# A ViT block with mixture of experts on one core: keys spread by ScalarE, value sums in column halves, a shorter routing chain, warm-up matmuls and a new order of steps

## The reference

```python
h = patches(x) @ W.T + b                           # 1152 tokens, 768 -> 192
# attn: a two-way time mix (wkv) and a channel mix
z = layernorm(h)
a = ln(z, w1, b1); k, v, sr = a @ Wk.T, a @ Wv.T, sigmoid(a @ Wr.T)
y = bi_wkv(decay / T, first / T, k, v)             # scans along the 36 tokens, both ways
z = z + (sr * y) @ Wo.T
c = ln(z, w2, b2)
h = h + z + sigmoid(c @ Wrf.T) * (square(relu(c @ Wkf.T)) @ Wvf.T)
# ffn: 12-head attention (head size 16), then 8 experts, the best 2 per token
z = layernorm(h); q, k, v = ln(z) @ qkv_w.T + qkv_b
z = z + softmax(q @ k.T / 4) @ v @ proj_w.T + proj_b
n = ln(z)
top, index = top_k(n @ w_gate, 2); gates = softmax(top)
moe = sum over the 2 experts e of gate * (gelu(n @ W1[e] + b1[e]) @ W2[e] + b2[e])
return h + z + moe
```

## Time and profile before

| | us |
|---|---|
| median of 3 runs (400.06, 400.08, 402.23) | 400.08 |
| the profiled execution | 396.91 |
| its span from first to last instruction | 395.1 |
| TensorE busy in the span | 319.4 |
| VectorE busy | 250.4 |
| ScalarE busy | 149.0 |
| GpSimd busy | 88.3 |

### The profile page before, as it was taken

The page is one execution under the profiler, slowest core; times in us unless marked ns, Lnnn a source line. Parts: engine busy times, 40 slices in busy tenths (PEclk is TensorE's granted clock), DMA queues, the critical chain, the costliest instruction groups (busy, mean ns, idle before and its releaser), DMA issues.

```text
span 395.1 us, 6068 instructions
## 1 busy us (share of the span) xinstructions
PE 319.4 (81%) x2039; PEld 287.0 (73%) x2039; DVE 250.4 (63%) x585; ACT 149.0 (38%) x352; POOL 88.3 (22%) x88
## 2 busy tenths in 40 slices
PE   3959901884798979999999998559299999999990
PEld 3948801573586958888898787548199999999980
DVE  1527998999899877675778898578413233322230
ACT  0054501331725056476824764230223333333320
POOL 9310002000110110110001000006405555555631
PEclk9989955576999999999999999658589999999996
DMA  8950000000000021243506687100402222222322
GB/s 271 359 150 2 1 0 0 2 0 0 1 2 1 0 64 32 70 152 108 151 15 200 168 219 220 40 2 0 120 21 42 42 40 41 41 40 41 51 24 22
DMA packets 20554, 27.25 MB, mean 69 GB/s; under 512 B 3458, under 2 KB 15570, under 8 KB 20522
## 3 DMA queue, kind: packets, MB, share of 16 engines
q1 hardware_dynamic: 16634, 22.80, 19.5%
q0 software_dynamic: 3888, 4.03, 6.9%
HBM read 22.05 MB, written 4.77 MB: 68 GB/s over the span
## 4 chain that ended last, share of the span: by engine, by line
PE 65%; DVE 18%; ACT 6%; issue 5%; DMA 3%; POOL 1%; DVEq 0%; SPq 0%; ACTq 0%; POOLq 0%
PE banks L1230 11%; PE banks L1231 10%; PE banks L1438 9%; PE banks L1427 7%; PE banks L1429 7%; PE banks L1300 6%; PE banks L1351 4%; PE banks L1253 3%; ACT ht L681 2%; PE banks L1324 2%; PE banks L1340 2%; PE banks L1263 1%; DVE patch L1144 1%; DMA patch<-in_xp 1%; DVE arena L921 1%
## 5 line engine op out<-in xcount | busy, mean ns | idle before, releaser
L574 POOL TENSOR_TENSOR rs<-va,consts 96x6 f32<-96x6 f32 (+1 forms) x16 | 18.1, 1132 | 221.5 <-DVEq L880 117.3
L1194 DVE TENSOR_SCALAR s<-banks,ffn 128x192 f32<-128x192 f32 x20 | 8.3, 417 | 57.4 <-PE banks L1438 57.1
L606 POOL DMA_INDIRECT out<-s,ffn x20 | 31.7, 1587 | 52.2 <-DVE s L1194 49.5
L821 ACT ACTIVATE ffn<-banks 128x384 f32<-128x384 f32 x40 | 19.6, 490 | 63.1 <-PE banks L1429 63.1
L1438 PE MATMUL banks<-arena,ffn 128*128 x240 | 42.1, 326 | 0.0
L1438 PEld LDWEIGHTS banks<-arena,ffn 128*128 128x128 f32 x240 | 38.5, 190 | 0.0
L1253 PE MATMUL banks<-arena,patch 128*96 128x192 f32 x144 | 25.9, 342 | 6.0 <-DMA patch<-in_xp 6.0
L1263 PE MATMUL banks<-consts,xh 96*128 96x96 f32 (+1 forms) x96 | 12.8, 279 | 21.8 <-DVEq L898 21.7
L1253 PEld LDWEIGHTS banks<-arena,patch 128*96 128x96 f32 x144 | 24.8, 173 | 6.7 <-issue 5.9
L1263 PEld LDWEIGHTS banks<-consts,xh 96*128 96x128 f32 (+1 forms) x96 | 10.7, 146 | 24.5 <-DVEq L898 23.3
L1230 PE MATMUL banks<-ht,kvrw 128*128 128x288 f32 x40 | 17.2, 518 | 12.3 <-ACT ht L681 6.4
(11 more groups left out here) (216 smaller groups left out, 766.7 us busy)
## 6 DMA issues: line engine op xcount, KB each, us to landing
arena<-in_w SPq DMA_DIRECT2D x8, 576.0 KB, 5.3
patch<-in_xp SPq DMA_DIRECT2D x12, 288.0 KB, 5.9
arena<-in_w1a SPq DMA_DIRECT2D x8, 384.0 KB, 3.9
vs<-v_scratch SPq DMA_DIRECT2D x24, 114.8 KB
arena<-in_w1b SPq DMA_DIRECT2D x8, 195.0 KB
v_scratch<-vt SPq DMA_DIRECT2D x4, 229.5 KB, 2.9
xh_scratch<-xh SPq DMA_DIRECT2D x4, 216.0 KB, 2.2
out<-h SPq DMA_DIRECT2D x1, 864.0 KB, 4.8
```

The costliest lines, as they stand in the source:

```text
L606: pool.indirect_dma_start(out[:, :], bass.IndirectOffsetOnAxis(ap=IS[:, j:j + 1], axis=0), YG[j % 2], None, compute_op=ALU.add).then_inc(s ...
L821: freed(A(HST[j % 2][:, 384 * i:384 * (i + 1)], ps[:, 0:384], ACT.Gelu), job)
```

## The change

- `spread` becomes `spread:b:g` on ScalarE: for each head one ACTIVATE from PSUM with scale = head mask (a column of `head0` or `head1`) and bias = KB, the masked key bias that VectorE computes once at the start. The key copies KT, `ke_ready` and VectorE's spread go; scores wait for the banks of k and qk1.
- `pv`: two matmuls per slab, one for each image, into the column halves; VectorE's `weighted` normalises both images at once.
- Routing: wider masks, sums in other layouts, rounding by adding and subtracting `WHOLE`, ranks accumulated in one PSUM region, RT in one operation, ONEB 8 rows by ScalarE and 16 in four wide operations by VectorE, GpSimd no longer takes part. The gather indices are written first, straight from PSUM, and have a semaphore of their own.
- `up`: the expert's number is loaded after the matmuls, not before.
- Four warm-up matmuls on zeros before the first tok.
- A new `ORDER`. Unused: `ON_ACT` stays empty, the `BY_ACT` lines don't change what runs.

```diff
 ORDER = """
 tok:0 tok:1 tok:2 stats:a:0 apply:a:0 tok:3 tok:4 tok:5 stats:a:1 apply:a:1 turn:a:0 kvr:0:0 turn:a:1 kvr:0:1 wkv:0:0
-kvr:2:0 wkv:0:1 wexp:0:0 kvr:1:1 wexp:0:1 wexp:0:2 wkv:0:2 kvr:1:0 wkv:0:3 wexp:0:3 wexp:0:4 wkv:0:4 wkv:0:5 tok:6
-tok:7 tok:8 tok:9 tok:10 kvr:2:1 tok:11 stats:a:2 stats:a:3 apply:a:2 apply:a:3 turn:a:2 kvr:0:2 turn:a:3 wkv:0:6
-kvr:0:3 wkv:1:0 wkv:1:1 wkv:1:2 wexp:1:0 wexp:1:1 wexp:1:2 wo:0 wo:1 kvr:1:3 kvr:2:2 kvr:2:3 hx:0 hx:1 stats:2:0
-apply:2:0 wexp:1:3 kvr:1:2 wkv:1:3 stats:2:1 turn:2:0 wkv:1:4 apply:2:1 wexp:1:4 wkv:1:5 kf:0:0 kf:1:0 rv:0 rv:1 rv:2
-wkv:1:6 ff:0 stats:b:0 turn:2:1 kf:0:1 kf:1:1 rv:3 rv:4 rv:5 apply:b:0 wo:2 wo:3 hx:2 hx:3 turn:b:0 vt:0 qk:0 vl:0:0
-vl:1:0 stats:2:2 apply:2:2 turn:2:2 kf:0:2 kf:1:2 stats:2:3 apply:2:3 turn:2:3 spread:0 s:0 exp:0 s:1 exp:1 ff:1 rv:6
...
+wkv:0:1 wexp:0:0 wexp:0:1 kvr:1:0 wexp:0:2 wexp:0:3 kvr:1:1 wkv:0:2 wexp:0:4 wkv:0:3 wkv:0:4 wkv:0:5 tok:6 tok:7 tok:8
+tok:9 tok:10 tok:11 stats:a:2 stats:a:3 apply:a:2 apply:a:3 kvr:2:0 kvr:2:1 wkv:0:6 turn:a:2 turn:a:3 kvr:0:3 kvr:0:2
+wkv:1:0 wo:0 wo:1 stats:2:0 hx:0 kvr:2:2 hx:1 wkv:1:1 wkv:1:2 apply:2:0 wexp:1:0 wexp:1:1 wexp:1:2 wexp:1:3 kvr:1:3
+kvr:1:2 wkv:1:3 turn:2:0 wexp:1:4 wkv:1:4 wkv:1:5 stats:2:1 kvr:2:3 kf:0:0 kf:1:0 rv:0 rv:1 apply:2:1 turn:2:1 wkv:1:6
+rv:2 ff:0 stats:b:0 apply:b:0 kf:0:1 kf:1:1 rv:3 wo:2 wo:3 turn:b:0 qk:0 spread:0:0 spread:1:0 hx:2 hx:3 stats:2:2
+apply:2:2 vt:0 vl:0:0 rv:4 rv:5 turn:2:2 s:0 exp:0 s:1 exp:1 vl:1:0 ff:1 stats:b:1 kf:0:2 kf:1:2 vm:0:0 pt:0 pt:1
...
         def _(act):
...
-                    if g:
-                        act.wait_ge(ke_ready, g)
-                    ps = full(act, ("k", g))
-                    freed(A(KT[:, 0, :], ps[:, 0:GT], ACT.Identity, bias=chan_("k_b", 0)), ("k", g))
                     ps = full(act, ("qk1", g))
                     A(QT[0:C1, g % 2, 1, 0:GT], ps[0:C1, 0:GT], ACT.Identity, bias=chan_("q_b", 1))
-                    freed(A(KT[0:C1, 1, :], ps[C1:2 * C1, 0:GT], ACT.Identity, bias=chan_("k_b", 1)), ("qk1", g))
+                if kind == "spread":
+                    b = step[1]
+                    heads, rows, lo, job = ((8, 128, 0, ("k", g)), (4, C1, C1, ("qk1", g)))[b]
...
+                    for h in range(heads):
+                        ins = A(ke[:, :, h, :], src, ACT.Identity, bias=KB[0:rows, 8 * b + h:8 * b + h + 1],
+                                scale=const_(f"head{b}", rows)[:, h:h + 1])
+                    freed(ins, job)
...
+            act.wait_ge(bb_ready, 1)
+            for i in range(NACT):
+                A(ONEB[:, i, :], const_("iota", T), ACT.Abs, bias=BB[:, i:i + 1], scale=-1.0).then_inc(apart_ready, 1)
+            for i in range(NACT):
+                act.wait_ge(apart_ready, i + 1)
+                A(ONEB[:, i, :], ONEB[:, i, :], ACT.Relu, bias=1.0, scale=-1.0).then_inc(table2_ready, 1)
...
         def _(dve):
...
+            dve.memset(O[:, :, :], 0.0).then_inc(warm_ready, 1)
...
+            dve.wait_ge(loaded["const"], 16)
+            for b, heads in ((0, 8), (1, 4)):
+                TS(KB[:, 8 * b:8 * b + heads], const_(f"head{b}"), CH[:, VAT["k_b"] + b:VAT["k_b"] + b + 1], None, ALU.mult).then_inc(kb_ready, 1)
...
             def weighted(p):
-                for a in range(2):
-                    r = slice(64 * a, 64 * a + 64)
-                    ins = TTR(O[r, p % 2, :].rearrange("p (h d) -> p h d", h=NH), ps[r, a, :, 0:HD],
-                              bc(RI[r, p % 2, :].unsqueeze(2), [64, NH, HD]), ALU.mult)
-                freed(ins, ("pv", p))
+                freed(TTR(O[:, p % 2, :].rearrange("p (h d) -> p h d", h=NH), ps[:, :, 0:HD],
+                          bc(RI[:, p % 2, :].unsqueeze(2), [128, NH, HD]), ALU.mult), ("pv", p))
...
+            ch.step(TTR(MK, bc(iota[:, 0:E].unsqueeze(1).unsqueeze(3), [T, 2, E, TILES]), bc(ixf.unsqueeze(2), [T, 2, E, TILES]), ALU.is_equal))
+            ch.step(TTR(M12, MK[:, 0], MK[:, 1], ALU.add))
+            dve.sem_inc(mask_ready, 1)
+            ch.step(dve.tensor_tensor_scan(CUM[:, :], const_("keep", T), M12[:, :], 0.0, ALU.mult, ALU.add))
+            ch.step(TTR(EXC, CUM, M12, ALU.subtract))
+            dve.sem_inc(mask_ready, 1)
...
+            ch.step(TS(AQ, SL, -63.5, WHOLE, ALU.add, ALU.add))
+            ch.step(TS(AQ, AQ, WHOLE, None, ALU.subtract))
+            ch.step(TTR(BB, SL, AQ, ALU.subtract))
             dve.sem_inc(bb_ready, 1)
...
+            TTR(RT.rearrange("p i (c a) -> p i c a", c=2), bc(AA.unsqueeze(2), [T, NC2, 2, MT]), bc(TG.unsqueeze(3), [T, NC2, 2, MT]),
+                ALU.mult).then_inc(rt_ready, 1)
+            for i in range(NACT, NC2, 4):
+                TTR(ONEB[:, i:i + 4, :], bc(iota.unsqueeze(1), [T, 4, 128]), bc(BB[:, i:i + 4].unsqueeze(2), [T, 4, 128]),
+                    ALU.is_equal).then_inc(table_ready, 1)
...
             ps = full(dve, ("list",))
+            TS(IG[:, :], ps[:, 0:MT], -1.0, 0.0, ALU.add, ALU.max).then_inc(list_ready, 1)
...
         def _(pe):
+            pe.wait_ge(warm_ready, 1)
+            for _ in range(WARM):
+                mm(banks[:, NBANK - 1, 0:2 * C], O[:, 0, 0:128], O[:, :, :].rearrange("p b c -> p (b c)"), start=True, stop=True)
...
-                        ins = mm(po[:, :, SW * s:SW * (s + 1)], PT[:, p % 2, 128 * s:128 * (s + 1)], VS[:, 2 * q:2 * q + 2, SW * s:SW * (s + 1)],
-                                 start=True, stop=True)
+                        for a in range(2):
+                            ins = mm(ps[64 * a:64 * a + 64, SW * s:SW * (s + 1)], PT[:, p % 2, 128 * s + 64 * a:128 * s + 64 * a + 64],
+                                     VS[:, 2 * q + a, SW * s:SW * (s + 1)], start=True, stop=True)
...
             def up(j):
-                if j < FULL:
-                    expert[j] = tile_expert(j)
                 taken(pe, ("xt", j))
...
                     end(ins, ("h", j, i))
+                if j < FULL:
+                    expert[j] = tile_expert(j)
```

More of the change, by code:

```diff
@@ new lines @@
+apply:b:1 rv:6 turn:b:1 vm:1:0 s:2 s:3 stats:2:3 apply:2:3 pv:0 pv:1 exp:2 qk:1 spread:0:1 rv:7 exp:3 rv:8 ff:2
+spread:1:1 pt:2 ot:0 pt:3 vt:1 turn:2:3 stats:b:2 s:4 ot:1 pv:2 pv:3 exp:4 kf:0:3 apply:b:2 turn:b:2 pt:4 kf:1:3 ot:2
+ot:3 vl:0:1 vl:1:1 vm:0:1 s:5 s:6 exp:5 qk:2 spread:1:2 exp:6 proj:0 stats:g:0 spread:0:2 apply:g:0 rv:9 vm:1:1 base:0
+rv:10 rv:11 ff:3 stats:b:3 turn:g:0 vt:2 logits:0 pt:5 s:7 exp:7 apply:b:3 pv:4 pv:5 vl:0:2 pt:6 s:8 pt:7 turn:b:3
+exp:8 s:9 exp:9 ot:4 pv:6 ot:5 pv:7 pt:8 pt:9 ot:6 vm:0:2 ot:7 qk:3 spread:0:3 spread:1:3 vl:1:2 proj:1 stats:g:1 s:10
@@ L106 @@
+vt:3 apply:g:1 turn:g:1 base:1 exp:10 vm:1:2 pv:8 s:11 exp:11 logits:1 pt:10 ot:8 pv:9 vl:0:3 s:12 pt:11 ot:9 pv:10
+pv:11 vl:1:3 s:13 exp:12 exp:13 pt:12 ot:10 s:14 ot:11 vm:0:3 pt:13 exp:14 s:15 exp:15 proj:2 pv:12 pv:13 vm:1:3
+stats:g:2 pt:14 pt:15 ot:12 pv:14 ot:13 pv:15 apply:g:2 base:2 ot:14 ot:15 proj:3 stats:g:3 turn:g:2 logits:2
+apply:g:3 turn:g:3 base:3 logits:3
 """
@@ L115 @@
 WKV_PARTS = 7
+WARM = 4
 ON_ACT = ""
@@ L1105, in _ @@
[L1105 to L1108 removed]
+            ch.step(dve.reciprocal(TG[:, 0:TILES, 1], DD[:, TILES:NC2]))
+            ch.step(TTR(TG[:, TILES:NC2, 1], TG[:, 0:TILES, 1], DD[:, 0:TILES], ALU.mult))
+            gf, gf2 = te(GF), te(GF2)
@@ L1109, in _ @@
+            ch.then(TTR(gf, MK[:, 0].rearrange("p e t -> p t e"), bc(TG[:, 0:TILES, 1].unsqueeze(2), [T, TILES, E]), ALU.mult))
+            ch.step(TTR(gf2, MK[:, 1].rearrange("p e t -> p t e"), bc(TG[:, TILES:NC2, 1].unsqueeze(2), [T, TILES, E]), ALU.mult))
+            ch.step(TTR(GF, GF, GF2, ALU.add))
             dve.sem_inc(gf_ready, 1)
             ps = full(dve, ("rank",))
+            ch.step(TS(TE[:, 0:E], ps[0:T, T:T + E], 63.5, WHOLE, ALU.add, ALU.add))
+            ch.step(TS(TE[:, 0:E], TE[:, 0:E], WHOLE, None, ALU.subtract))
@@ L1112, in _ @@
+            ch.step(dve.tensor_tensor_scan(END[:, 0:E], const_("ones", T)[:, 0:E], TE[:, 0:E], 0.0, ALU.mult, ALU.add))
+            ch.step(TTR(BASE[:, 0:E], END[:, 0:E], TE[:, 0:E], ALU.subtract))
             et = lambda x: x.rearrange("p (e t) -> p e t", e=E)
-            ch.step(CP(et(TOTC[:, :]), ps[0:T, T:2 * T].rearrange("p (t e) -> p e t", e=E)))
-            ch.step(dve.tensor_tensor_scan(CUM[:, :], const_("keep", T), TOTC[:, :], 0.0, ALU.mult, ALU.add))
-            ch.then(CP(NE8[:, 0:E], et(CUM[:, :])[:, :, TILES - 1]))
@@ L1379, in _ @@
             ps = begin(("rank",))
-            mm(ps[0:T, 0:T], const_("before", T), M12[:, :], start=True, stop=True)
-            end(mm(ps[0:T, T:2 * T], const_("ones", T), M12[:, :], start=True, stop=True), ("rank",))
+            mm(ps[0:T, 0:TILES * E], const_("before", T), M12[:, :], start=True, stop=False)
+            pe.wait_ge(mask_ready, 2)
+            mm(ps[0:T, 0:TILES * E], const_("ones", T), EXC[:, :], start=False, stop=True)
```

(1 more changed line is left out.)

146 lines of the change are left out of this document (43 added, 103 removed).

## The result

The changed kernel takes 395.19 us (median of 390.62, 394.64, 395.74 and 395.83) against 400.07 for the kernel before, a ratio of 0.9865 with a 95% interval of 0.9818 to 0.9913: 4.9 us gained where 10.2 were forecast. The profiled execution took 395.83 (before 396.91), its span is 393.9 (before 395.1).

A forecast was written before the change was run, and what follows sets the result against it. VectorE was taken to bound the scans, TensorE the channel mix, attention and expert tiles. Start -2.3, scans 0, attention -4.6 and routing -3.3 sum to -10.2 us: 389.9 us forecast, range 381 to 397.5.

The forecast's parts named there:

- the clock at the list: Rival (d), routing: the 48 list instructions find TensorE at half pace, +5.5 us, 395.5 in all; chance 0.07.
- The rest: DMA loads, last projection to logits, expert tiles, last scatter: load places and instructions stay the same, 0 (+-0.5) us.
- Value sums as halves: Attention stretch: column halves run beside each other on TensorE, 0.55 us per pair instead of 0.89, -5.4 us.
- 0.99 per pair: Estimate in rival (b), halves don't pay: 62 ns per matmul makes value sums +1.6 us, 396.9 in all; rival's chance 0.12.
- Spread and order: Attention stretch: ScalarE's key spread +1.0 us, receptance work moved behind the scans +3.2, TensorE waits filled by it -2.7.
- rv:4 and rv:5: Receptance steps placed behind wo:2 and wo:3: 3.2 us moves into the TensorE-bound stretch, filling waits worth 2.7.
- Rival (a): Attention stretch: ScalarE becomes the bound, TensorE stands through each group's eight-head block, 15.6 us, 404.5 in all; chance 0.08.
- signs that I gave for being wrong: Halves over 0.9 us per pair, TensorE waiting for spread rows by name, or first scan staying at 32.
- Start: Before the first scan: warm-up matmuls let tile 0 run at full pace, -2.3 us (bounds 0 and -3.6).
- Scans: Time-mix scans, 32.3 to 132.5 us: same VectorE instructions in nearly the same order, 0 us (-1.5 to +1).
- Routing: Routing start to first gather: list start and length +0.3, gather indices written at once from PSUM -1.6 us.
- Register load: Before the first up matmuls: moving the expert number's load behind them removes a 1.81 us pause, -2.0 with the turn's tail.

The follow-up runs named there:

- e7: The kernel before with only the changed kernel's step order, key spread still on VectorE: 412.2 us, ratio 1.0337 to the kernel before.
- e12: The kernel before with the experts' weights asked for in the gaps between its value reloads: 399.8 us, ratio 1.0018 to the kernel before.
- e13: The changed kernel with the routing chain of before, register load still behind the up matmuls: 397.0 us, ratio 0.9955 to the kernel before.
- e2: The changed kernel with the experts' weights asked for in the gaps between the value reloads: 388.7 us, ratio 0.9698 to the kernel before.
- e4: The changed kernel with the old whole-width value sums and their normalising in two operations: 396.6 us, ratio 0.9965 to the kernel before.
- e8: e2 with the old whole-width value sums and their normalising in two operations: 396.2 us, ratio 0.9933 to the kernel before.
- e9: e2 with the key spread back on VectorE, in the same step order: 396.9 us, ratio 0.9960 to the kernel before.
- e1: The changed kernel with the old step order, ScalarE's spread directly behind each qk step: 412.6 us, ratio 1.0330 to the kernel before.
- e10: e2 with the second group's channel mix started earlier and rv:4, rv:5 before wo:2: 392.4 us, ratio 0.9853 to the kernel before.
- e6: The changed kernel with the expert number's register load back before the first up matmuls: 396.8 us, ratio 0.9911 to the kernel before.

## Why the prediction was right, and where it was off

- *Range and sign.* Faster, by 1.35% and inside 381 to 397.5. The size was half of what I gave, and no rival describes it: the nearest by number, the clock at the list (395.5), did not happen: the 48 list instructions took 5.5 us in both profiles. It did happen in three kernels with the old routing (e7, e12, e13), which I had not thought of.
- *The step that failed* is "The rest": "the value loads (vl) and the experts' weights keep their place among the steps around them ...: 0". I compared only the last weights with the first expert tile. In the new order the weights of three experts are asked for within 9 us around the third group's reload, and one expert's right before the fourth's. Price: 6.5 us (e2), which with the 4.9 gained makes 11.4, against the 10.2 forecast. That nearness is partly luck. With the weights clear the attention stretch is 111.9 us, 0.4 under the kernel before and not 4.6: the reloads explain 3.7 of the 7.9 us missing there, and the rest is in the two points on the value sums and on spread and order.
- *Value sums as halves*, -5.4: TensorE's time for them fell by 5.6 us (0.58 per pair against 0.55 taken, and 0.54 in e2, where no pair ran at the lower clock). The mechanism and the price were right; what reached the time is what e4 and e8 show. Two pairs' 32 instructions start at 228.23 and the next group at 229.29, 1.06 / 32 = 33 ns each. The Trainium skill (TensorE: Matmul & The Clock Gate, section Back-to-back issue gap) gives about 62 ns per matmul, on which I built 0.99 per pair, for the case that hardware decode is off, and a floor of about 25 ns otherwise. The 33 ns rule the first case out here and agree with the second.

```profile
228.23 1.26 PE L1335 MATMUL banks<-vs,pt 108*64 108x51 f32 x32
229.29 0.70 PE L1308 MATMUL banks<-patch,qt 128*64 128x288 f32 x4
```

- *Spread and order.* I summed +1.0 for the spread, +3.2 for rv:4 and rv:5, and -2.7 for filled waits, as if each had its own price. The runs show one edit in three parts: spread on ScalarE -7.3 of the stretch in the new order (e9), the order -18.5 with that spread and +13.0 without it (e1, e7), the moved receptance work +4.9 of TensorE's time as its cover (e10). Their sum, with the whole sums and the weights clear, is 117.1 against 112.3 before (e8): +4.8, where I had +1.5 before the halves (3.2 - 2.7 + 1.0); against e12, the kernel before with the weights clear, it is +2.8. So this term was too small by 1 to 3 us. Rival (a), ScalarE as the bound, is what e1 shows, 412.6; its mechanism was real and the new order is what kept it away.
- *Signs.* Of the signs that I gave for being wrong one shows, small: TensorE waits by name for the spread rows, once for 1.3 us (L757, above). The halves at 0.58 us per pair, the first scan at 30.8 and TensorE's idle time of 6.7 us up to 243.6 came as said.
- *Start* -2.3: -1.5 at the first scan; the clock's fall, which I left open, moved later instead of away. *Scans* 0: -1.1 in this profile, within my bound; the stretch reads 98.9 to 99.1 us in nine of the kernels with the new order and 100.0 to 100.2 in the three with the old one, so it is the order's (e10, whose order differs here, and e13 are the exceptions with 99.9 and 100.3).
- *Routing* -1.3 up to the gather: -1.4 in the two profiles, where the list ran at the same clock, -2.6 by e13, where it did not. *Register load* -2.0: -2.2 from gather to up, but e6 gives it 0.9. I took 1.8 from a single row; with the load in the same place e7, e12 and e6 have 6.0, 6.0 and 6.1 us from gather to up against that profile's 7.4.

The kernel with the weights clear is the best version found: 388.7 us, 3.0% (2.0 to 4.0) under the kernel before and 1.7% under the changed one by the ratios.
